# Gathers two steps ahead, zeroing from SyncE, reordered first loads, shorter lags for the last sequences, and the tiles' expert weights on ScalarE's DMA queue

## What is computed

```python
x = x + tanh(g_xattn[0]) * L0_xattn(ctx, layernorm(x), mask, ...)   # 8 heads; keys: 375 of ctx, 112 latents
x = x + tanh(g_ffn[0])   * L0_ffn(layernorm(x), ...)                # 8 experts, the best 2 of each token
x = x + tanh(g_xattn[1]) * L1_xattn(ctx, layernorm(x), mask, ...)   # 16 heads, same keys and latents
x = x + tanh(g_ffn[1])   * L1_ffn(x, ...)                           # int8 activations, ternary weights, conv, silu
```

## Time and profile before

| | before |
|---|---|
| median of 3 runs | 1647.11 us (1629.59, 1647.11, 1647.48) |
| profiled execution | 1629.14 us, its span 1627.4 us |
| busy PE / DVE / ACT / POOL | 1300.2 (80%) / 1052.1 (65%) / 982.5 (60%) / 1111.9 (68%) us |
| granted TensorE clock, mean | 0.922 of full speed |
| moved by DMA | 239.96 MB, mean 147 GB/s |

### The profile page before, as it was taken

One profiled execution on the slowest core, in us unless ns is written; L12 is line 12 of the kernel. 1 busy time (PEld: TensorE's weight loads), 2 busy tenths in 40 slices (PEclk: granted clock), 3 DMA queues, 4 the chain that ended last, 5 costly groups with the idle time before them and its releaser, 6 DMA issues.

```text
span 1627.4 us, 45130 instructions
## 1 busy us (share of the span) xinstructions
PE 1300.2 (80%) x16918; PEld 1010.2 (62%) x16918; DVE 1052.1 (65%) x2819; ACT 982.5 (60%) x2319; POOL 1111.9 (68%) x1365
## 2 busy tenths in 40 slices
PE   1667778768888978879989998898889888977962
PEld 0345556547767756657778786676666666656651
DVE  4368778886556645755666666776667666766763
ACT  2478677655556665555546556676667666766741
POOL 3567777786666764475767677677768676767775
PEclk9789889989999989889999999999999999999995
DMA  4898888397999844377999995334454344534420
GB/s 133 251 178 226 223 198 211 77 218 165 245 237 247 206 87 85 84 188 164 234 245 226 249 246 115 91 73 88 88 86 82 81 87 91 86 75 83 84 60 6
DMA packets 443130, 239.96 MB, mean 147 GB/s; under 512 B 388785, under 2 KB 425761, under 8 KB 434337
## 3 DMA queue, kind: packets, MB, share of 16 engines
q1 hardware_dynamic: 407100, 172.49, 51.6%
q10 hardware_dynamic: 32740, 57.24, 11.0%
q0 software_dynamic: 3072, 7.34, 1.5%
HBM read 107.78 MB, written 35.50 MB: 88 GB/s over the span
## 4 chain that ended last, share of the span: by engine, by line
PE 34%; POOL 20%; DVE 11%; DMA 11%; ACT 8%; issue 8%; SPq 2%; DVEq 2%; ACTq 2%; POOLq 0%
PE bank_ring L1051 8%; POOL probs L623 6%; PE bank_ring L1037 5%; PE bank_ring L1089 4%; PE bank_out L1070 4%; DVE scores L1299 4%; DMA expert_up<-experts_up 4%; DMA raw_weights<-moe_results,route_slots 3%; PE bank_scores L1011 3%; PE bank_x L1150 2%; DMA probs_turned<-probs 2%; ACT scores L815 2%; PE bank_x L1103 2%; ACT values L842 2%; PE bank_x L1024 2%
## 5 line engine op out<-in xcount | busy, mean ns | idle before, releaser
L623 POOL TENSOR_TENSOR probs<-scores,probs 112x487 f16<-112x487 f32 x384 | 424.2, 1120 | 305.9 <-ACT probs L822 301.0
L815 ACT ACTIVATE scores<-scores,score_min 112x487 f32<-112x487 f32 x384 | 265.8, 693 | 142.3 <-DVE score_min L1299 136.9
L1316 DVE SCALAR_TENSOR_TENSOR values<-bank_ring,values 128x512 f16<-128x512 f32 x192 | 132.4, 689 | 249.1 <-ACT values L842 247.5
L1299 DVE CUSTOM_DVE_ANT_0 scores<-bank_scores,mask 112x487 f32<-112x487 f32 x384 | 238.2, 658 | 2.5 <-PE bank_scores L1011 2.3
L822 ACT ACTIVATE probs<-scores 112x487 f16<-112x487 f32 x384 | 213.9, 604 | 26.1 <-DMA probs_turned<-probs 10.3
L842 ACT ACTIVATE values<-bank_ring 128x512 f16<-128x512 f32 x192 | 113.5, 591 | 185.7 <-PE bank_out L1070 148.6
L1051 PE MATMUL bank_ring<-weights,kv_B 128*128 128x128 f16 x3072 | 207.3, 228 | 0.6 <-DVE keys L1311 0.6
L1051 PEld LDWEIGHTS bank_ring<-weights,kv_B 128*128 128x128 f16 x3072 | 196.2, 103 | 10.7 <-DVE keys L1311 1.1
L1070 PE MATMUL bank_out<-values,probs_turned 128*128 128x64 f16 x4608 | 174.7, 196 | 30.6 <-issue 17.1
L1070 PEld LDWEIGHTS bank_out<-values,probs_turned 128*128 128x128 f16 x4608 | 162.4, 100 | 35.1 <-issue 24.3
L1037 PE MATMUL bank_ring<-kv_B,weights 128*128 128x488 f16 x768 | 181.9, 373 | 0.3 <-issue 0.3
(11 more groups left out here) (226 smaller groups left out, 2448.2 us busy)
## 6 DMA issues: line engine op xcount, KB each, us to landing
expert_up<-experts_up SPq DMA_DIRECT2D x43, 1024.0 KB
expert_down<-experts_down SPq DMA_DIRECT2D x43, 512.0 KB
raw_weights<-in_weights ACTq DMA_DIRECT2D x8, 1536.0 KB, 10.4
experts_up<-expert_up ACTq DMA_DIRECT2D x8, 1024.0 KB, 5.1
raw_weights<-in_weights ACTq DMA_DIRECT2D x6, 1024.0 KB, 7.2
probs_turned<-probs SPq DMA_TRANSPOSE x384
context_turned_B<-kv_B ACTq DMA_DIRECT2D x16, 375.0 KB, 7.3
kv_B<-context_turned_B ACTq DMA_DIRECT2D x16, 375.0 KB, 3.7
```

The source lines that it names most:

```text
L623: pool.tensor_tensor(PR[:, u % 4, 1, 0:KEYS], S[:, u % 4, 0:KEYS], PR[:, u % 4, 0, 0:KEYS], ALU.subtract).then_inc(probs_split, 1)
L815: act_e.activation(S[:, u % 4, 0:KEYS], S[:, u % 4, 0:KEYS], ACT.Exp, bias=rmin[:, u % 4:u % 4 + 1], scale=-1.0, accum_out=rsum[:, g % 2, ...
L1299: dve.tensor_tensor_reduce(out=S[:, u % 4, 0:KEYS], in0=bS[u % 2][0:TOK, 0:KEYS], in1=mask[:, m, 0:KEYS], scale=1.0, scalar=3.0e38, op0=AL ...
L1316: dve.scalar_tensor_tensor(vN[:, j % 2, 1].rearrange("p t d -> p (t d)"), bank("v", j)[:], 1 / WSCALE, vN[:, j % 2, 0].rearrange("p t d -> ...
```

## The change

1. `gather(n)` stands two steps before `combine(n)` instead of one, but for sequences 0 and 6.
2. The zeros for `moe_rows` go out from SP at the start, in 5 transfers whose rows are 5 to 10 KB per partition, instead of 2 transfers of 1 KB rows from ACT in step 0; all ten slots of `xr` are set to zero for it, and the first `m_turn` waits for it.
3. SP issues context 1 and `X[:, 1]` right behind the small loads, then the rest of `X`, without waiting. DVE no longer starts with the gates (now in step -8), `p_apply` stands ahead of the next sequence's statistics, and the split of layer 0's weights moves from steps -9, -8 to -6, -5. The first two expert loads move from step 0 to step -3.
4. On POOL the halves of `split_context(n, ., 0)` move ahead of each `split_probs` of their step, and `round_context` on ACT moves one step earlier. For sequence 0 the layer 0 parts come before the layer 1 parts.
5. `load_expert` moves from SP to ACT, between `round_k` and the first `round_hidden`.
6. The distances of F become a table: shorter for sequences 14 and 15 (`F_QUICK`), slightly for 13 (`F_MIDDLE`). For sequence 15 the second half of `conv_sides` and of `f_scale` and the rounding of that half run on DVE.

```diff
+ZERO_DMAS = sum(-(-t // XR_SLOTS) for t in TILES)
...
+F_STEPS = {"stats": 13, "rstd": 14, "rows": 15, "round": 16, "turn": 16, "up0": 17, "up1": 18, "sides0": 19,
+           "sides1": 20, "tanh0": 19, "tanh1": 20, "act0": 20, "act1": 21, "max0": 20, "max1": 21, "rate": 22,
+           "scale0": 23, "scale1": 24, "down": 26, "store": 27}
+LAST_HALF = (NSEQ - 1, 1)
+F_QUICK = {"stats": 13, "rstd": 13, "rows": 13, "round": 13, "turn": 13, "up0": 14, "up1": 15, "sides0": 16,
+           "sides1": 17, "tanh0": 16, "tanh1": 17, "act0": 17, "act1": 18, "max0": 17, "max1": 18, "rate": 19,
+           "scale0": 20, "scale1": 21, "down": 22, "store": 23}
+F_MIDDLE = {**F_STEPS, "stats": 13, "rstd": 14, "rows": 14, "round": 15, "turn": 15, "up0": 16, "up1": 17,
+            "sides0": 18, "sides1": 19, "tanh0": 18, "tanh1": 19, "act0": 19, "act1": 20, "max0": 19, "max1": 20,
+            "rate": 22, "scale0": 23, "scale1": 24}
+
+
+def f_step(n, name):
+    return start_b(n) + (F_QUICK if n >= NSEQ - 2 else F_MIDDLE if n == NSEQ - 3 else F_STEPS)[name]
...
-        if j == start_b(n) + 26:
+        if j == f_step(n, "down"):
             tasks.append(("f_down", n))
+        if n == NSEQ - 3 and j == f_step(n, "rate"):
+            tasks.append(("f_rate", n))
...
-            sp.wait_ge(x_loaded, 16)
-            sp.dma_start(X[:, 1:NSEQ], x_in[1:NSEQ].rearrange("n t d -> t n d")).then_inc(x_loaded, 16)
+            sp.dma_start(ctxb[0:CP, 1], ctx_in[1].rearrange("(t p) d -> p t d", p=CP)).then_inc(ctx_loaded[1], 16)
+            sp.dma_start(X[:, 1], x_in[1]).then_inc(x_loaded[1], 16)
+            sp.dma_start(X[:, 2:NSEQ], x_in[2:NSEQ].rearrange("n t d -> t n d")).then_inc(x_loaded[2], 16)
+            sp.wait_ge(zeros_set, 1)
+            for b in range(2):
+                rows = xs[b].rearrange("(p t) c -> p (t c)", p=128)
+                for at in range(0, TILES[b] * 2 * DIM, XR_SLOTS * 2 * DIM):
+                    n = min(XR_SLOTS * 2 * DIM, TILES[b] * 2 * DIM - at)
+                    sp.dma_start(rows[:, at:at + n], xr[:].rearrange("p s c -> p (s c)")[:, 0:n])\
+                        .then_inc(rows_zeroed, 16)
...
-                if (j + 3) % 4 == 0 and 0 <= (j + 3) // 4 < NSEQ:
+                if (j + 4) % 4 == 0 and 0 < (j + 4) // 4 < NSEQ:
+                    split_context((j + 4) // 4, 0, 0)
+                if j == -5:
+                    split_context(0, 0, 0)
+                    split_context(0, 1, 0)
+                    split_latents(0, 0)
+                    split_context(0, 0, 1)
+                    split_context(0, 1, 1)
+                if (j + 3) % 4 == 0 and 0 < (j + 3) // 4 < NSEQ:
                     split_latents(0, (j + 3) // 4)
                 for t in late(j - 2):
-                    if t[0] == "p_turn":
+                    if t[0] == "p_turn" and t[1]:
                         split_context(t[1], t[2], 1)
                     if t[0] == "b_lat":
                         split_latents(1, t[1])
                 for n in range(NSEQ):
-                    at = j - start_b(n)
-                    if at in (19, 20):
-                        conv_sides(n, at - 19)
-                    if at in (23, 24):
-                        f_scale(n, at - 23)
-                    if at == 24:
-                        f_round(n)
+                    for i in range(2):
+                        if (n, i) != LAST_HALF and j == f_step(n, f"sides{i}"):
+                            conv_sides(n, i)
+                    for i in range(2):
+                        if (n, i) != LAST_HALF and j == f_step(n, f"scale{i}"):
+                            f_scale(n, i)
+                            if i == 1 or n == NSEQ - 1:
+                                f_round(n)
                 if is_pair(j):
                     split_probs(2 * j)
                 m = micro(j)[0]
                 if m:
                     split_hidden(m[1], m[2], m[3])
-                if (j + 4) % 4 == 0 and 0 <= (j + 4) // 4 < NSEQ:
-                    split_context((j + 4) // 4, 0, 0)
+                if (j + 4) % 4 == 0 and 0 < (j + 4) // 4 < NSEQ:
+                    split_context((j + 4) // 4, 1, 0)
                 if is_pair(j):
                     split_probs(2 * j + 1)
-                if (j + 4) % 4 == 0 and 0 <= (j + 4) // 4 < NSEQ:
-                    split_context((j + 4) // 4, 1, 0)
                 for b in range(2):
                     first = SCATTERS[b] * (j - routed(b) - 3)
                     for n, k in scatters(b)[max(first, 0):max(first + SCATTERS[b], 0)]:
                         scatter(b, n, k)
                 for n in range(NSEQ):
-                    if j == combine_step(n) - 1:
+                    if j == combine_step(n) - (1 if n in (BATCHES[0][0], BATCHES[1][0]) else 2):
                         gather(n)
...
+            def load_expert(b, i, part):
+                t = tile(b, i)
+                if i == 0 and part == 0:
+                    act_e.wait_ge(slots_ready, b + 1)
+                    act_e.wait_ge(ex_stored[0], 32 * 4)
+                    act_e.wait_ge(ex_stored[1], 32 * 4)
+                e = act_e.value_load(ids[b][0:1, i:i + 1], min_val=0, max_val=EXPERTS - 1)
+                if part == 0:
+                    if t >= 2:
+                        act_e.wait_ge(up_ready, 2 * (t - 2) + 2)
+                    act_e.dma_start(eup[:, t % 2], up_dram[e]).then_inc(up_loaded[t % 2], 16)
+                else:
+                    if t >= 2:
+                        act_e.wait_ge(x0_filled, X0_AT[("down",) + ((b, i - 2) if i >= 2 else (0, TILES[0] - 2 + i))])
+                    act_e.dma_start(edown[:, t % 2], down_dram[e]).then_inc(down_loaded[t % 2], 16)
+
             def load_weights(j):
-                if j == 0:
+                if j == -3:
                     act_e.wait_ge(l0_split, L0_CHUNKS)
                     load_raw(2, 0, 6, weights_in, L0_CHUNKS)
                     load_raw(3, 1, 6, weights_in, L0_CHUNKS + MOE_CHUNKS)
-                    act_e.wait_ge(zeros_set, 1)
-                    for b in range(2):
-                        act_e.dma_start(xs[b].rearrange("(t p) c -> p t c", p=128),
-                                        xr[:, XR_SLOTS - 1:XR_SLOTS, :].to_broadcast([128, TILES[b], 2 * DIM]))\
-                            .then_inc(rows_zeroed, 16)
...
                 if is_pair(j + 2):
                     round_k(j + 2)
+                for b in range(2):
+                    i = j - first_tile_step(b)
+                    if i == -3:
+                        load_expert(b, 0, 0)
+                        load_expert(b, 0, 1)
+                        load_expert(b, 1, 0)
+                        load_expert(b, 1, 1)
+                    if 2 <= i + 1 < TILES[b]:
+                        load_expert(b, i + 1, 0)
+                    if 2 <= i < TILES[b]:
+                        load_expert(b, i, 1)
                 if m[0]:
                     round_hidden(m[0][1], m[0][2], m[0][3])
...
+                if (j + 5) % 4 == 0 and 0 <= (j + 5) // 4 < NSEQ:
+                    round_context((j + 5) // 4)
                 if (j + 4) % 4 == 0 and 0 <= (j + 4) // 4 < NSEQ:
-                    round_context((j + 4) // 4)
...
-            dve.memset(xr[:, XR_SLOTS - 1], 0.0)
+            dve.memset(xr[:], 0.0)
...
+            def conv_sides(n, j):
+                dve.wait_ge(conv_begun, 2 * n + j + 1)
+                for tap in (1, 2):
+                    if tap == 2:
+                        dve.drain()
+                    for i in range(4):
+                        b = 4 * j + i
+                        c = V_CONVW + FB * tap + b
+                        last = dve.scalar_tensor_tensor(hacts[n % 2][:, b, :], hpads[j][:, i, tap:tap + TOK],
+                                                        vec[:, c:c + 1], hacts[n % 2][:, b, :], ALU.mult, ALU.add)
+                last.then_inc(conv_last, 1)
+
+            def f_scale(n, j):
+                h = hacts[n % 2][:, 4 * j:4 * j + 4, :]
+                dve.tensor_tensor(h, h, rate2.rearrange("p (o t) -> p o t", o=1).to_broadcast([128, 4, TOK]), ALU.mult)
+                dve.drain()
+                dve.tensor_scalar(h, h, ROUND, None, ALU.add)
+                dve.drain()
+                dve.tensor_scalar(q2T[:, 4 * j:4 * j + 4], h, ROUND, None, ALU.subtract).then_inc(q2_last, 1)
```

119 lines of the change are left out of this document (55 added, 64 removed).

## The result

The changed kernel takes 1594.19 us (median of 4 runs, 1585.56 to 1612.41) against 1646.11 us of the kernel before; the ratio is 0.969 with a 95% interval of 0.960 to 0.978. It is faster, as forecast, but by 52 us and not by 124, and lies 36 us above the upper end of the range (1558). The profiled execution took 1594.61 us, its span 1592.8.

A forecast was written before the change was run, and what follows sets the result against it. It took most of the kernel to be bound by engines waiting for one another. Gains of 128 us less 4 gave 1505 us from the profiled 1629.1, raised to 1512 for the uncertain median; range 1475 to 1558 us.

The forecast's parts named there:

- gathers: At combine, mostly phase B: issuing a step earlier removes 12 of DVE's 14 waits for gathered rows; -62 us, bounds 25 and 75.
- start: Before step 0: context 1 issued early and layer 0 halves first bring PE's first projection forward; -12 us, bounds 5 and 15.
- zeros: Step 0: the zeros' issues no longer hold ACT for 10.28 us, on SP nobody waits; -14 us, bounds 9 and 20.
- mask waits of phase A: New sequences' preparation: POOL's new order brings the mask about 3.5 us earlier for PE; -20 us, bounds 5 and 31.
- expert loads: Tile steps: issued on ACT, upper weights go out some 4 us sooner; -12 us, bounds 0 and 25, +4 for ACT's issues.
- tail: Sequence 15's end: DVE takes half of POOL's convolution and scaling; -8 us, bounds 3 and 15, shorter distances counted as nothing.
- the transfer of these ... stays where it was: Tile steps: the rows' transfer, issued at 457.64, is unmoved and PE waits for it too, so only 12 of 19.5 us go.
- two signs named for the error: Tile steps: PE waiting for `raw_weights<-moe_rows` and ACT idling by "issue" would show the forecast wrong; no size given.
- The rival with the other sign: 43 tile steps: ACT becomes the bound, its issues held by a full queue; 1770 us at 6 us a step; chance 0.03.
- the start's bound: Start: the lower bound of 5 us gain, if zeros and `X` crowd out the loads.
- the sign that I named: New sequences in phase A: PE's wait for the mask, 41.0 us before, would fall under 15 us.
- The rival in which POOL becomes the bound: Phase B: POOL, nearly full in the combine's two steps, limits the gathers to 25 us instead of 62; 1549 us; chance 0.15.

The follow-up runs named there:

- b_gather2: The kernel before with only its gathers issued one step earlier: 1561.4 us, ratio 0.951.
- y_zeros_act: y_tables_old with the zeros back on ScalarE in step 0, in two transfers of 1 KB rows: 1532.2 us, ratio 0.940.
- y_pool_old: y_tables_old with POOL's order of context splits and ACT's place of the context rounding put back for sequences 1 to 15: 1549.5 us, ratio 0.949.
- y_pool_half: y_tables_old with the last half of sequence 15's convolution, scaling and rounding back on POOL: 1529.4 us, ratio 0.933.
- y_tables_old: The changed kernel with its expert loads back on SP and F's old distances for all sequences: 1523.9 us, ratio 0.934.

## Why the prediction was wrong, step by step

| term | predicted | measured | by |
|---|---|---|---|
| gathers | -62 | -76 (-53 by the traces) | b_gather2, medians |
| start | -12 | -6 | 49.0 to 42.9 us, y_zeros_act |
| zeros | -14 | 0 | 87.9 against 88.1 us |
| mask waits of phase A | -20 | -26 (-14 by the traces) | y_pool_old |
| expert loads | -12 + 4 | **+48** | ratios with and without |
| tail | -8 | **+12** | -4.5 and +16.3 us |

**Expert loads**: the step that failed is "the transfer of these ... stays where it was". It dealt with the rows' issue, which did stay; but their transfer, which took 3.6 us by the median, took 6.6 with 1.5 MB per tile in ScalarE's queue instead of their own, and PE waited 61.5 us for them. I had taken the queue for a waiting line only. The forecast that PE's wait for `expert_up` falls under 8 us came true, as did two signs named for the error, PE waiting for the rows and ScalarE idling by "issue". The rival with the other sign had the right place and the wrong mechanism: no issue took over 0.7 us. ScalarE's idle 28.8 us are 1.1 us in 26 of the 43 tile steps, where I had counted 4 steps; what share of the loss they are is not separated. The Trainium skill's rule that I weighed (DMA: Bandwidth & Descriptors, Issuing engines are not separate DMA queues: several issuing engines save only the sequencer's time), with a term of 0, was no closer: these runs measured a loss of 48.

**Tail**: what failed is that I counted the shorter distances "as nothing". Distances are slack; I costed the work that they move and not the waits that they had kept apart. DVE's half was given 8 us, all that it takes off POOL by busy time; 4.5 came. Between sequence 15's first `f_up` and its `f_down`, by the traces of y_pool_half and y_tables_old, the scaling gives 3.5 of them and the convolution 1.0, as DVE does its half of that ahead of its own product for the first half.

**Start and zeros** were costed as two terms, each with the other absent. Zeros at the start were said to delay nobody, but context 2, which nobody waits behind in SP's order, waits for the engines' time. I had the price in the start's bound ("zeros and `X` crowd out the loads") and not in the sum. Steps 0 to 5 are 11 us shorter even with the zeros in step 0 (45.2, not 56.3), for which I had no term. ScalarE's queue in the kernel before, then in y_zeros_act:

```profile
51.74 1.96 ACTq L739 DMA_DIRECT2D raw_weights<-in_weights  x2
53.74 10.28 ACTq L771 DMA_DIRECT2D moe_rows<-moe_rows  x2
```
```profile
45.72 3.79 ACTq L804 DMA_DIRECT2D moe_rows<-moe_rows  x2
```

The same issues of zeros hold ScalarE for 3.79 us, where the two weight loads no longer stand right ahead of them. So the 10.28 us that I gave to the zeros were in good part the price of those loads, which the change moved to step -3; no run moves them alone.

**New sequences**: the size came near, the sign that I named did not: PE's wait for the mask fell only to 33.7 us, not under 15. In y_tables_old it is 27.3, in y_pool_old 47.8; these 20.5 us are the part's worth in waits, and the gain in time is 14 by the traces, 26 by the medians.

**Gathers**: mechanism right, size too small in phase B (60.9 us, not 51), elsewhere not to be told from the variation. Two steps around a combine take 11.4 us at clock 1.00, not 12.6: the 1.3 us that I allowed for the next sequence's statistics were not needed. PE's busy time in them falls from 13.38 to 10.88 us by the clock. The rival in which POOL becomes the bound is out.

**Sum**: with the measured sizes the forecast of 1512 becomes 1512 + 56 + 20 + 6 + 14 - 14 - 6 = 1588 us, and with the 11 us of steps 0 to 5 1577. The forecast started from a kernel of 1512 + 124 = 1636 us, the median is 1646; that leaves 7 us, less than the tile steps vary. Part of this closeness is luck: with the traces' sizes for the gathers and the mask waits, from the profiled execution's 1629.1, the terms give about 1606, not 1594.6. Two terms that I gave 16 us of gain carry 76 of the miss, and neither had a range that reached across zero by its mechanism: for the expert loads I had set "bounds 0 and 25", with up to 47 us for ScalarE's issues alone. (The gathers' own working, 51 + 12, gives 63, not 62.)

## What to carry to other kernels

A transfer that another engine issues is not the same transfer. Ask what the transfers on the other queues (here transposes and gathers) take to land with it, and what the issuing engine's own order loses; in this kernel, bulk loads cost less in the queue in which the transposes stand. Fixed distances between steps of a chain are what keeps engines in order from waiting for each other; shortening them lost time here, for the last sequence too. A wait of 5 us in an engine that is in order costs more than itself where the clock falls behind it, and one line that issues a load a step earlier can outweigh an elaborate rearrangement.

## What the runs showed of the hardware

- The same 1 MB loads cost the kernel 0.32 us each in the transposes' queue and 0.70 us in ScalarE's, issues included, at DMA shares of 1.06 and 1.05. A quarter of the packet size changed that to 0.64.
- Gathers in a third queue landed in 3.2 us without these loads, in 4.8 with them in SP's queue, and in 7.8 with them in ScalarE's.
- A transpose that takes 1.2 to 1.3 us to issue took 13.63 us for two, with loads of the other queue under way; the share of DMA's time was then no sign of throughput: 181 GB/s at 1.20 in 389 to 409 us.

```profile
389.00:409.00 20.00, 7.20 (x102) 5.55 (x99) 8.50 (x19) 6.24 (x15) 7.91 (x11) 0.81 1.20 181
```

- In steps 104 to 185 of b_gather2 the granted clock went from 0.95 to 1.00 once the waits for gathered rows had gone, and PE's busy time for the same products from 466.09 to 446.90 us.
